# A fused attention and gated feed-forward layer: gate and up multiplied side by side on the two row halves of TensorE, low-rank factors stacked on 96 rows, one background step per attention slot

## The chip, the cores and the metric

One NeuronCore of one Trainium2 chip runs the program. The metric is the device time of one execution in microseconds. Times quoted for the kernel before are those of three timed runs and of one profiled execution.

## What is computed

The input x has 2 x 1024 tokens of width 512, all in float32. Cut to what matters:

```python
xn = _layernorm(x)
# attention: 32 heads of 16 channels, 8 key/value groups, causal
s = softmax(mask(q @ k.T) / 4) @ v @ Wo + bo
# feed-forward, every matrix with a low-rank part of rank 16
gate   = xn @ gate_w.T + (xn @ gate_a.T) @ gate_b.T      # 512 -> 1376
up     = xn @ up_w.T   + (xn @ up_a.T)   @ up_b.T
hidden = silu(gate) * up
g = silu(hidden @ down_w.T + (hidden @ down_a.T) @ down_b.T)
out = x + s * g
```

## The kernel before

Two streams of work are written out for each engine and merged by `interleave`. The *attention* stream goes in slots: 40 slots (`SLOTS`) for each of 16 groups (`N`), a leading round of 40 and 16 last slots. A slot's number within its round decides what stands in it. At each even slot TensorE computes a pair of transposed score tiles `st` (`scores_t`, L887), which ScalarE turns into probabilities `prob` (L1092), one per slot; mostly at even slots it also computes a pair of score tiles `s` (`score_pair`, L868), of which VectorE takes row maxima (L1318, L1321). Both kinds use two matmuls side by side, one on the upper and one on the lower 64 rows of the array. `context` (L904) multiplies probabilities by values, four heads side by side on 32 columns each; it stands at six of the ten slots of a round whose number leaves 2 when divided by 4.

The *background* stream is all the rest, cut into 777 steps (`STEPS`, `TOTAL`). A step of a projection, of gate or up, of down or out is one 128-row tile of the contraction: three matmuls of 128x128 by 128x512 (L197 to L199 in `matmul_hi_lo`), since every operand is split into a high and a low part of type float32r. The stages are: turning x, projections, `b_turn` (the low-rank b factors are transposed), then for each of 11 tiles of hidden rows (`NH`) a `fold` (weights transposed on TensorE, L755, and the product of the low-rank factors added, L759, then split into `w_hi` by ScalarE, L974, and `w_lo` by VectorE, L1173) and `gate` and `up` for each of four chunks of 512 tokens; then `down_fold` (L784, L788), and 16 times `down` (11 steps) and `out` (4 steps). The gate tile is read by `tanh` (ScalarE, L989) and by `gate` (VectorE, L1184); the up tile by `up` (VectorE, L1195), which writes `hid`.

The background has two PSUM banks. A bank goes to units by turn: unit u takes bank u % 2, and `take_bank` waits until unit u - 2 has been read out. So the next gate is computed in one bank while the last up stands in the other.

`interleave` issues an attention slot and then background steps until a quota is met; `MIDDLE` steps are spread evenly over 640 slots (584 steps, 0.91 a slot), after which one step goes with each of the 16 last slots, and the rest follows with no attention beside it. In the second half of the tokens an `out` stands between two `down`s, as in the first half. `load_out` issues nine DMAs on SyncE's queue (L537, L538, L541) into three buffers; `combine` (L1235, L1238), an add on GpSimd (L438) and a store (L545) end a tile.

## Time and profile before

| | |
|---|---|
| median of three runs | 1152.95 us (1144.7 to 1156.6) |
| profiled execution: time, span | 1163.04 us, 1161.2 us |
| granted TensorE clock, mean | 0.923 |
| TensorE busy | 1056.7 us (91%) |
| TensorE weight loads busy | 607.1 us (52%) |
| VectorE busy | 631.7 us (54%) |
| ScalarE busy | 464.8 us (40%) |
| GpSimd busy | 115.3 us (10%) |

The profiled execution is 10 us longer than the median of the timed ones. Weight loads run beside matmuls and are counted apart. A matmul's record runs on after the next has begun, so the distance between two starts is the price of one, not its length.

### The profile page before, as it was taken

The page shows a single profiled execution, that of the slowest core. Times are in us where ns is not written, and L with a number is a line of the kernel's source. Part 1 is how long each engine was busy: PE and PEld are TensorE (multiplying, and loading weights), DVE is VectorE, ACT ScalarE, POOL GpSimd, SP SyncE. Part 2 cuts the span into 40 slices and gives each one's busy share as a digit, 9 for nine tenths or more (in the row PEclk, how much of TensorE's full clock was granted, in tenths as well). Part 3 has the DMA queues.
Part 4 walks back from the last instruction along what each step waited for, and adds up shares of the span by engine and source line. Part 5 has one row for each costly group of instructions (what it writes and reads, how often), then busy time and mean ns, then how long its engine had stood idle before and what let it go on. Part 6 is the DMA issues. An engine that isn't in the chain of part 4 may idle for free.

```text
span 1161.2 us, 16175 instructions
## 1 busy us (share of the span) xinstructions
PE 1056.7 (91%) x5668; PEld 607.1 (52%) x5668; DVE 631.7 (54%) x1752; ACT 464.8 (40%) x917; POOL 115.3 (10%) x159
## 2 busy tenths in 40 slices
PE   4749997999999999999999999999878878799897
PEld 3535453555555555555555555554344434456685
DVE  6636453565655565655665565565545545432344
ACT  3312343544544444444444453444433324353121
POOL 3000000010000101010100000010000101112011
PEclk9979796999999999999999998997678879899899
DMA  6435344131321313130312223124031242133552
GB/s 190 136 108 192 124 148 133 42 91 39 92 75 55 84 36 92 38 87 30 91 54 76 70 60 86 39 75 137 29 95 46 61 115 72 47 102 97 157 166 97
DMA packets 118862, 103.49 MB, mean 89 GB/s; under 512 B 41352, under 2 KB 86408, under 8 KB 118784
## 3 DMA queue, kind: packets, MB, share of 16 engines
q1 hardware_dynamic: 118784, 102.47, 29.5%
q8 instruction: 46, 0.75, 0.3%
q14 instruction: 32, 0.26, 0.1%
HBM read 60.20 MB, written 41.42 MB: 88 GB/s over the span
## 4 chain that ended last, share of the span: by engine, by line
PE 79%; DVE 7%; DMA 5%; ACT 4%; SPq 3%; issue 2%; POOL 0%; POOLq 0%; DVEq 0%; ACTq 0%
PE bank L197 17%; PE o L904 12%; PE bank L198 12%; PE bank L199 12%; PE st L887 11%; PE s L868 8%; DMA q<-scratch_q 2%; PE bank L759 2%; ACT prob L1092 2%; DMA hid_in<-scratch_hid 2%; PE bank L788 1%; PE bank L725 1%; PE bank L755 1%; DVE junk L1318 1%; PE bank L784 1%
## 5 line engine op out<-in xcount | busy, mean ns | idle before, releaser
L1092 ACT ACTIVATE prob<-st 128x512 f32<-128x512 f32 (+1 forms) x640 | 328.1, 551 | 454.6 <-PE st L887 454.2
L1318 DVE CUSTOM_DVE_ANT_0 junk<-s,mask 128x128 bf16<-128x128 f32 (+3 forms) x512 | 230.3, 488 | 208.1 <-PE s L868 207.2
L1321 DVE TENSOR_REDUCE part_max<-s 128x1 f32<-128x512 f32 x256 | 164.8, 686 | 138.6 <-PE s L868 138.4
L868 PE MATMUL s<-k,q 64*128 64x512 f32 (+3 forms) x768 | 153.2, 394 | 42.7 <-DMA q<-scratch_q 25.6
L887 PE MATMUL st<-q,k 64*128 64x512 f32 (+3 forms) x768 | 158.4, 436 | 17.6 <-ACT prob L1092 16.0
L427 POOL TENSOR_SCALAR_AFFINE_SELECT prob<-prob 128x512 f32<-128x512 f32 x128 | 79.8, 635 | 891.3 <-ACT prob L1092 891.3
L197 PE MATMUL bank<-x_hi,w_hi 128*128 128x512 f32 (+1 forms) x352 | 162.7, 462 | 0.0
L904 PE MATMUL o<-prob,v 128*32 128x512 f32 (+3 forms) x1536 | 158.8, 535 | 0.0
L887 PEld LDWEIGHTS st<-q,k 64*128 64x128 f32 x768 | 69.4, 191 | 139.1 <-issue 90.0
L199 PE MATMUL bank<-x_hi,w_lo 128*128 128x512 f32 (+1 forms) x352 | 138.9, 395 | 0.0
L198 PE MATMUL bank<-x_lo,w_hi 128*128 128x512 f32 (+1 forms) x352 | 138.6, 394 | 0.0
L868 PEld LDWEIGHTS s<-k,q 64*128 64x128 f32 x768 | 78.6, 198 | 86.8 <-DVE part_max L1318 30.5
L197 PEld LDWEIGHTS bank<-x_hi,w_hi 128*128 128x128 f32 (+1 forms) x352 | 65.5, 186 | 77.6 <-issue 66.5
L197 PE MATMUL bank<-down_hi,hid_hi 128*128 128x512 f32 (+1 forms) x176 | 80.1, 455 | 7.7 <-DVE ring L1219 5.8
L904 PEld LDWEIGHTS o<-prob,v 128*32 128x32 f32 x1536 | 41.5, 115 | 75.2 <-issue 67.4
L199 PEld LDWEIGHTS bank<-x_hi,w_lo 128*128 128x128 f32 (+1 forms) x352 | 65.4, 186 | 16.1
L198 PE MATMUL bank<-down_lo,hid_hi 128*128 128x512 f32 (+1 forms) x176 | 73.1, 415 | 0.0
L199 PE MATMUL bank<-down_hi,hid_in_lo 128*128 128x512 f32 (+1 forms) x176 | 72.4, 411 | 0.0
L198 PEld LDWEIGHTS bank<-x_lo,w_hi 128*128 128x128 f32 (+1 forms) x352 | 65.7, 187 | 5.4
L197 PEld LDWEIGHTS bank<-down_hi,hid_hi 128*128 128x128 f32 (+1 forms) x176 | 35.3, 200 | 31.4 <-issue 22.4
L1318 DVE DVE_READ_ACCUMULATOR2_ANT part_max<- 128x1 f32 x512 | 42.5, 83 | 0.0
L1184 DVE SCALAR_TENSOR_TENSOR gated<-tanh,bank 128x512 f32<-128x512 f32 (+1 forms) x44 | 30.0, 682 | 21.5 <-ACT tanh L989 21.2
(103 smaller groups left out, 962.1 us busy)
## 6 DMA issues: line engine op xcount, KB each, us to landing
q<-scratch_q SPq DMA_DIRECT2D x64, 200.0 KB
scratch_hid<-hid SPq DMA_DIRECT2D x40, 256.0 KB, 2.1
hid_in<-scratch_hid SPq DMA_DIRECT2D x16, 640.0 KB, 4.3
scratch_q<-proj_hi SPq DMA_DIRECT2D x32, 256.0 KB
scratch_o<-o_sb SPq DMA_DIRECT2D x32, 256.0 KB, 2.1
k<-scratch_k SPq DMA_DIRECT2D x32, 192.0 KB
scratch_q<-proj_lo SPq DMA_DIRECT2D x16, 256.0 KB
ctx<-scratch_o SPq DMA_DIRECT2D x64, 64.0 KB
```

Of the source, the lines that this page charges most:

```text
L197: pe.matmul(out, lhs_hi, rhs_hi, start=start, stop=False)
L198: pe.matmul(out, lhs_hi, rhs_lo, start=False, stop=False)
L199: return pe.matmul(out, lhs_lo, rhs_hi, start=False, stop=stop)
L427: ins = pool.affine_select(out=blk, in_=blk, compare_op=ALU.is_ge, fill=0.0, base=0, pattern=[[0, REP], [1, P]], channel_multiplier=-1)
L759: mm = pe.matmul(out_[:, kt * P:kt * P + hp], a_gu[:, i, kt * P:(kt + 1) * P], bT[:, i, h * P:h * P + hp], start=False, stop=kt == KT - 1, ...
L868: pe.matmul(sb_[(p + odd) % S_BANKS][:, 0:wd], q[half, g % 2, h // 2, qt * P:(qt + 1) * P], k[half, g % 2, k0:k0 + wd], start=True, stop=T ...
L887: mm = pe.matmul(st[odd][:, col:col + q1 - q0], k[half, i % 2, kt * P:(kt + 1) * P], q[half, i % 2, h // 2, q0:q1], start=True, stop=True)
L904: mm = pe.matmul(ob[32 * h:32 * h + 2 * HD, q0 % C:q0 % C + q1 - q0], v[:, i % 3, kt].rearrange("p a e -> p (a e)"), prob[:, job % 3, h, c ...
L1092: nc.scalar.activation(prob[:, job % 3, h, 0:JOB_COLS[j]], st[at % ST_BANKS][:, 0:JOB_COLS[j]], ACT.Exp, scale=float(HD) ** -0.5).then_inc ...
L1184: dve.scalar_tensor_tensor(out=gated[0:hp], in0=th[0:hp], scalar=1.0, in1=bank_of(key)[0:hp, :], op0=ALU.add, op1=ALU.mult).then_inc(gated ...
L1318: ins = dve.tensor_tensor_reduce(junk[:, n % S_BANKS, 0:wd], bank_[:, 0:wd], mask[:, C - wd:C], 1.0, LOWEST, ALU.add, ALU.max, part[:, h, ...
L1321: ins = dve.tensor_reduce(part[:, h, qt, dst:dst + 1], bank_[:, 0:wd], AX.X, ALU.max)
```

## The change

`gate` and `up` of a chunk become one unit `hidden` of eight steps that holds both banks. In the first four steps the upper 64 rows of each contraction tile are multiplied by gate weights into bank 0 while the lower 64 rows are multiplied by up weights into bank 1; in the last four the halves are crossed over. Each step is three pairs of matmuls with 64 rows. ScalarE and VectorE begin to read when all eight steps are done, and `take_bank` of the next unit waits for what was last in its bank or banks (`PRIOR`).

The low-rank factors are loaded three times, at rows 0, 32 and 64 of 96: a as high, low, high and b as high, high, low, so that one float32r matmul with 96 rows gives what one float32 matmul with 16 rows gave. New work for this: a clearing and six copies on GpSimd, `split_a` and `split_b` on ScalarE, `low_a` and `low_b` on VectorE, ten small loads where there were six.

`MIDDLE` is 640 now, one step in each slot, and 69 steps are left behind the middle, where there were 125. VectorE issues a slot's background before its attention. The `out`s of the second half stand behind all `down`s, with `load_out` three tiles ahead.

```diff
@@ bank_order, interleave
-            yield "gate", h, c
-            yield "up", h, c
+            yield "hidden", h, c
...
-        elif t >= NT // 2 + 2:
-            yield "out", t - 2, 0
-    for t in range(NT - 2, NT):
+    for t in range(NT // 2, NT):
         yield "out", t, 0
...
-TAIL = LAST_SLOTS + STEPS["down"] * (NT // 2 - 1) + STEPS["out"] * NT // 2
-MIDDLE = TOTAL - LEAD - EARLY - TAIL
+MIDDLE = SLOTS * N
+TAIL = TOTAL - LEAD - EARLY - MIDDLE
...
+        if kind == "hidden":
+            used = (0, 1)
+        else:
+            used, turn = (turn,), 1 - turn
+        places[kind, a, b] = used
+        prior[kind, a, b] = sorted({last[n] for n in used} - {None})
@@ tensor
             def take_bank(key):
-                u = NUMBER[key]
-                if u >= 2:
-                    pe.wait_ge(*read_out(*KEYS[u - 2]))
-                return bank[u % 2]
+                for u in PRIOR[key]:
+                    pe.wait_ge(*read_out(*KEYS[u]))
+                return bank_of(key)
...
-                for kt in range(KT):
-                    mm = matmul_hi_lo(pe, out_[0:hp, :], wh[:, h % 2, i, kt, 0:hp], wl[:, h % 2, i, kt, 0:hp],
-                                      xh[:, c, kt], xl[:, c, kt], kt == 0, kt == KT - 1)
...
+                take_bank(("hidden", h, c))
+                for cross in range(2):
+                    if cross:
+                        pe.wait_ge(crossed, NCH * h + c + 1)
+                    for kt in range(KT):
+                        for w_, x_ in ((wh, xh), (wl, xh), (wh, xl)):
+                            for odd in range(2):
+                                i = odd ^ cross
+                                half = head_rows(odd, HALF_ROWS)
+                                mm = pe.matmul(bank[i][0:hp, :], w_[half, h % 2, i, kt, 0:hp], x_[half, c, kt],
+                                               start=not cross and kt == 0 and w_ is wh and x_ is xh,
+                                               stop=cross == 1 and kt == KT - 1 and x_ is xl)
...
-                pe.matmul(out_[0:hp, :], a_low[:, h * P:h * P + hp], bT_d[:, :], start=False, stop=True,
+                pe.matmul(out_[0:hp, :], a_d[:, h * P:h * P + hp], bT_d[:, :], start=False, stop=True,
@@ sync
+                for t in range(NT // 2, NT // 2 + 3):
+                    load_out(t)
+                for t in range(NT // 2, NT):
                     yield STEPS["out"]
                     store_out(t)
+                    if t + 3 < NT:
+                        load_out(t + 3)
@@ vector
-            interleave(attention(), background())
+            interleave(attention(), background(), background_first=True)
```

**Where the order moves.** TensorE between one chunk and the next, seventh tile of hidden rows. Before, the up steps (bank1) end and the gate of the next chunk (bank0) begins:

```order
L197 MATMUL bank1<-x_hi,w_hi 128x512
L198 MATMUL bank1<-x_lo,w_hi 128x512
L199 MATMUL bank1<-x_hi,w_lo 128x512
L868 MATMUL s2<-k,q 128x256 [waits s_read]
L868 MATMUL s0<-k,q 128x256
L197 MATMUL bank0<-x_hi,w_hi 128x512 [waits gated_done]
L198 MATMUL bank0<-x_lo,w_hi 128x512
L199 MATMUL bank0<-x_hi,w_lo 128x512
```

The same place now:

```order
L835 MATMUL bank1<-x_lo,w_hi 128x512
L835 MATMUL bank0<-x_lo,w_hi 128x512
L951 MATMUL st0<-q,k 128x512 [waits exp_done]
L951 MATMUL st1<-q,k 128x512
L932 MATMUL s2<-k,q 128x128 [waits s_read]
L932 MATMUL s0<-k,q 128x128
L835 MATMUL bank0<-x_hi,w_hi 128x512 [waits hid_done]
L835 MATMUL bank1<-x_hi,w_hi 128x512
L835 MATMUL bank0<-x_hi,w_lo 128x512
```

The wait before the first matmul of a chunk is now for `hid`, the last reading of the chunk just ended, where it was for the gate reading of that chunk, four steps old; only an `st` pair and an `s` pair (and at some places a `context`) stand between.

ScalarE at the same place, before:

```order
L1092 ACTIVATE prob<-st1 128x512 [waits st_done]
L1110 ACTIVATE o_sb<-o 128x512 [waits sums_landed1,o_stored1,pv_done]
L989 ACTIVATE tanh<-bank0 128x512 [waits gated_done,filled]
L1092 ACTIVATE prob<-st0 128x512 [waits pv_done,st_done]
L1092 ACTIVATE prob<-st1 128x512 [waits st_done]
```

and now:

```order
L1170 ACTIVATE prob<-st1 128x512 [waits st_done]
L1170 ACTIVATE prob<-st0 128x512 [waits st_done]
L1062 ACTIVATE tanh<-bank0 128x512 [waits gated_done,filled]
L1170 ACTIVATE prob<-st1 128x512 [waits st_done]
L1170 ACTIVATE prob<-st0 128x512 [waits pv_done,st_done]
```

The `tanh` stands behind the exponential of `st0`, and that `st0` is the one that TensorE computes after the chunk's last matmul.

VectorE in the last stage, where tiles of the second half are finished. Before, between two `down`s:

```order
L1210 TENSOR_TENSOR hid_in_lo<-hid_in,hid_hi 128x1280 [waits hh_done]
L1211 TENSOR_TENSOR hid_in_lo<-hid_in,hid_hi 96x128
L1219 SCALAR_TENSOR_TENSOR ring<-y_tanh,bank0 128x512 [waits out_stored4,yt_done]
L1224 TENSOR_TENSOR ctx<-ctx,inv_sums 128x512 [waits c_landed2]
L1228 TENSOR_TENSOR ctx_lo<-ctx,ctx_hi 128x512 [waits ch_done]
L1235 TENSOR_TENSOR r1<-bank1,bias 128x512 [waits r2_done,filled]
L1238 SCALAR_TENSOR_TENSOR ring<-r1,ring 128x512 [waits y_done,r1_done]
```

and now, behind the last `down`:

```order
L1315 SCALAR_TENSOR_TENSOR ring<-y_tanh,bank1 128x512 [waits out_stored7,yt_done]
L1320 TENSOR_TENSOR ctx<-ctx,inv_sums 128x512 [waits c_landed2]
L1324 TENSOR_TENSOR ctx_lo<-ctx,ctx_hi 128x512 [waits ch_done]
L1320 TENSOR_TENSOR ctx<-ctx,inv_sums 128x512 [waits c_landed0]
L1324 TENSOR_TENSOR ctx_lo<-ctx,ctx_hi 128x512 [waits ch_done]
L1331 TENSOR_TENSOR r1<-bank0,bias 128x512 [waits r2_done,filled]
L1334 SCALAR_TENSOR_TENSOR ring<-r1,ring 128x512 [waits y_done,r1_done]
L1320 TENSOR_TENSOR ctx<-ctx,inv_sums 128x512 [waits c_landed1]
```

The eight `out`s now follow one another with no `down` (11 steps of TensorE) between them.

## Rows read from the trace of the kernel before

**Rows 1.** The page, part 1: busy time and instructions of each engine.

```profile
PE 1056.7 (91%) x5668; PEld 607.1 (52%) x5668; DVE 631.7 (54%) x1752; ACT 464.8 (40%) x917; POOL 115.3 (10%) x159
```

**Rows 2.** Windows by stage: start:end, length; busy (count) by engine; clock; DMA.

```profile
0.00:106.00 106.00, 67.58 (x335) 50.84 (x335) 62.96 (x168) 29.13 (x53) 9.02 (x15) 0.90 0.48 143
106.00:211.00 105.00, 92.61 (x469) 49.76 (x470) 49.74 (x162) 42.10 (x87) 7.47 (x12) 0.82 0.44 142
211.00:788.00 577.00, 572.58 (x3379) 316.28 (x3379) 346.38 (x1045) 263.64 (x537) 54.16 (x87) 0.99 0.23 66
788.00:842.00 54.00, 50.00 (x191) 20.34 (x191) 29.27 (x74) 25.23 (x45) 2.49 (x4) 0.64 0.29 88
842.00:1061.00 219.00, 186.45 (x930) 99.14 (x929) 101.83 (x251) 85.52 (x168) 27.84 (x31) 0.86 0.27 79
1061.00:1161.20 100.20, 87.46 (x373) 70.75 (x369) 41.48 (x58) 19.14 (x29) 14.27 (x10) 0.95 0.44 134
```

**Rows 3.** Timeline, gate steps and attention: start, duration, engine, line, operands.

```profile
504.39 0.50 PE L197 MATMUL bank<-x_hi,w_hi 128*128 128x512 f32 x1
504.73 0.40 PE L198 MATMUL bank<-x_lo,w_hi 128*128 128x512 f32 x1
504.96 0.40 PE L199 MATMUL bank<-x_hi,w_lo 128*128 128x512 f32 x1
...
505.29 0.50 PE L887 MATMUL st<-q,k 64*128 64x512 f32 x2
505.39 0.19 PEld L868 LDWEIGHTS s<-k,q 64*128 64x128 f32 x2
505.62 0.40 PE L868 MATMUL s<-k,q 64*128 64x512 f32 x2
...
505.95 0.50 PE L197 MATMUL bank<-x_hi,w_hi 128*128 128x512 f32 x1
...
510.34 0.30 PEld L887 LDWEIGHTS st<-q,k 64*128 64x128 f32 x4 [0.36 <-issue]
```

**Rows 4.** Timeline, the readings that follow a filled tile, at two places.

```profile
456.64 0.50 PE L887 MATMUL st<-q,k 64*128 64x384 f32 x4
...
457.18 0.60 ACT L1092 ACTIVATE prob<-st 128x512 f32<-128x512 f32 x1 [1.25 <-PE st L887]
...
457.67 0.59 ACT L989 ACTIVATE tanh<-bank 128x512 f32<-128x512 f32 x1
...
458.30 0.69 DVE L1184 SCALAR_TENSOR_TENSOR gated<-tanh,bank 128x512 f32<-128x512 f32 x1 [1.76 <-ACT tanh L989]
...
789.72 0.68 DVE L1195 SCALAR_TENSOR_TENSOR hid<-gated,bank 96x512 f32<-96x512 f32 x1
...
790.54 0.63 PE L784 MATMUL bank<-ident,ring 128*128 128x128 f32 x4 [0.88 <-DVE hid L1195]
```

**Rows 5.** Timeline, `context` of one block of 256 columns and of two of 512.

```profile
508.18 0.64 PE L904 MATMUL o<-prob,v 128*32 128x256 f32 x8
...
907.43 1.92 PE L904 MATMUL o<-prob,v 128*32 128x512 f32 x16
```

**Rows 6.** Timeline, low-rank products of a fold and of a down fold.

```profile
503.31 1.15 PE L759 MATMUL bank<-bT,a_low 16*128 16x128 f32 x8
...
801.40 1.12 PE L788 MATMUL bank<-bT_d,a_low 16*128 16x512 f32 x2
```

**Rows 7.** Timeline, TensorE behind idle times in the down stage.

```profile
872.21 0.79 PE L868 MATMUL s<-k,q 64*128 64x512 f32 x2 [7.23 <-DVE part_max L1318]
...
918.53 0.73 PE L868 MATMUL s<-k,q 64*128 64x512 f32 x2 [1.81 <-DVE part_max L1318]
```

**Rows 8.** Timeline, loading and readying a tile of the last stage.

```profile
1082.29 0.69 DVE L1224 TENSOR_TENSOR ctx<-ctx,inv_sums 128x512 f32<-128x512 f32 x1 [2.48 <-DMA x_again<-in_L_attn_x]
...
1131.62 0.59 SPq L537 DMA_DIRECT2D ctx<-scratch_o  x1
...
1136.59 0.46 SPq L541 DMA_DIRECT2D x_again<-in_L_attn_x  x1
```

More of the change, by code:

```diff
@@ L94 @@
 PROJECTED += AFTER
-STEPS = dict(turn=1, proj=KT, value=TT, b_turn=1, fold=2, gate=KT, up=KT, down_fold=2, down=NH, out=KT)
+DOWN_LOADED, DOWN_SPLIT, DOWN_TURNED = 1, 3, NH - 1
+STEPS = dict(turn=1, proj=KT, value=TT, b_turn=1, fold=2, hidden=2 * KT, down_fold=2, down=NH, out=KT)
 def bank_order():
@@ L138 @@
 NUMBER = {key: u for u, key in enumerate(KEYS)}
+NUMBER_STEPS = dict(zip(KEYS, accumulate(STEPS[kind] for kind, *_ in KEYS)))
 TOTAL = sum(STEPS[kind] for kind, *_ in NUMBER)
@@ L150, in interleave @@
         done += next(background)
-    for slot, _ in enumerate(attention):
+    if not background_first:
+        next(attention)
+    for slot in range(SLOTS * (N + 1) + LAST_SLOTS):
         if slot < SLOTS:
@@ L159, in interleave @@
             done += next(background)
+        next(attention, None)
     for _ in background:
@@ L444, in background @@
                         add(t - 1)
-                    elif t >= NT // 2 + 2:
-                        yield STEPS["out"]
-                        add(t - 2)
-                for t in range(NT - 2, NT):
+                for t in range(NT // 2, NT):
                     yield STEPS["out"]
@@ L833, in background @@
                     for c in range(NCH):
-                        for i in range(2):
-                            yield from hidden(h, c, i)
+                        yield from hidden(h, c)
                         if c == 1 and h + 1 < NH:
@@ L978, in tanh @@
             def tanh(h, c):
-                key = ("gate", h, c)
+                key = ("hidden", h, c)
                 hp = rows[h]
```

255 lines of the change are left out of this document (162 added, 93 removed).

## The prediction

> **What bounds the kernel now.** I read the busy times first: TensorE is busy for 91% of the span, no other engine for more than 54% [rows 1]. Then the windows by stage [rows 2]: from 211 to 788, the gate and up stage, TensorE is busy 572.6 of 577 us at a clock of 0.99, so there every nanosecond of TensorE counts and every wait of it is new time. From 842 to 1061 (downs beside attention) it is busy 186 of 219 us at 0.86, and there latencies bind. Then the timeline shows what a switch costs [rows 3]. Full-height matmuls follow one another every 0.23 us (504.73 to 504.96). From the last of them to the 64-row `st` pair it takes 0.33 (504.96 to 505.29), from that pair to the next pair 0.33, from the `s` pair back to a full matmul 0.33, and from that first one to the second 0.33. So each change between kinds of tile costs 0.1 us at the end of the old kind and 0.1 at the start of the new. Pair to pair there is no change, and a pair costs what a full matmul does.
>
> **The gate and up stage.** I count it from the order of the program. Before: 1053 full matmuls at 0.228 (240 us); 514 attention pairs of 384 columns on the average, at 0.18 (93); 129 context groups at 0.66 (85), from 0.64 less two changes for 256 columns and 0.86 for 512 [rows 5]; 20 folds at 0.44 for the turning and 1.08 for the low-rank product [rows 6] (30); 2 us of turned maxima. That is 450. The stage has 577, of which 4.4 are idle and 6 lost to the clock; the other 117 are spread on 604 changes of kind, 0.19 each, as the rows say.
>
> After, the same stage has 1054 pairs in place of the full matmuls. A pair in a row of pairs has no row here longer than two; I bound it between 0.21 (512 columns as fast as they stream) and 0.33 (nothing overlapped), and take 0.228, since the loads for the `s` pair start at 505.39, 0.1 us into the `st` pair, and four loads for two pairs end within 0.30 us [rows 3]: 240 us. Attention, with 47 fewer slots of it in this stage since a slot now carries a whole step: 466 pairs (84), 116 groups (77). Folds: the product on 96 rows lies between 0.23 and the old 1.08; I take 0.44, the price of the four transposes, which also use 128 columns each: 18 us. Maxima 2. Changes of kind: 187 are left in the order, at 0.19: 35. Sum 456.
>
> **The new wait.** A chunk holds both banks, so the next one waits until the last reading of this one is over. The order shows what stands between: `st`, `s`, at some places `context`. The chain of readings, from the start of that `st` pair [rows 4]: exponential after 0.54 (0.43 where no change stands ahead), `tanh` 0.49 later (the exponential stands before it on ScalarE), gate 0.63 later, 0.69 for it, `hid` 0.68 and 0.14 until TensorE starts (789.72 to 790.54). Sum 3.06 us. Against this TensorE has 0.3 to 0.6 us of pairs, and 0.6 to 1.9 of context where there is one. Of 44 ends of a chunk, 16 have only pairs: 2.6 us of idle each, 41 us. Four have the context of 256 columns: 1.7 each, 7. The other 24 have longer ones: 13 together. Behind a fold the chain is shorter by one reading (2.4 us), and 11 such places add 9. Together 70 us. Queued behind that wait are all later `st` and `s` pairs, so ScalarE and VectorE wait too, but both have room. With 5 us of the old idle time the stage comes to 531.
>
> **The clock.** At 918.53, behind 1.81 us of idle, the `s` pair takes 0.73 instead of 0.40 [rows 7, 3]: TensorE went from 2.4 to 1.2 GHz, and what it does in such a stretch takes twice as long; I price one fall at 1.7 us. The new 2.6 us waits are longer. Against that speaks that dense pairs stand around them. I take six of ten of the 16 bare waits (16 us) and 10 us for the folds, where waits and transposes come together: 26, between 0 (no fall) and 55 (one at each of 33 places). Stage after: 556, before 577.
>
> The Trainium skill, "TensorE: Matmul & The Clock Gate", in "Why this matters for your kernels", warns only of idle gaps longer than the waits I forecast; by it this term would be nil. The trace has a fall behind a shorter gap, so the term stays.
>
> **The other stages.** Up to 106 nothing changes. Projections (106 to 211): five slots of attention fewer, 1 us each: 100. Down folds (788 to 842, clock 0.64): 11 products fall from 1.05 [rows 6] to 0.23 at full clock, 9 us, and to 15 with the clock as it is there: 39. Downs beside attention: 173 steps instead of 117, so 168 more matmuls (38 us), 56 more pairs (10), 14 more groups (9), 65 more changes (12). By the same prices the stage before had 162 us of work in 219, so 57 were lost for 8.6 tiles: ScalarE and VectorE stand in order behind the landing of `hid_in`, at worst 7.23 us [rows 7]. Now 12.4 tiles, the later ones with fewer duties; I add 18, between 0 and 25. VectorE's background ahead of its attention may help or harm there; nothing excludes either, and I take 0 of a band of 15 each way. Stage after: 219 + 69 + 18 = 306.
>
> **The end.** Behind the last context (1061) before: 100 us for 123 steps. After: 35 steps are left, but how they follow matters. Three tiles are loaded ahead; each of the other five loads takes 5.4 us of SyncE's queue (1131.62 to 1137.05) and 0.44 for the store ahead of it, lands 2.3 us later, and then takes 2.1 us in VectorE and ScalarE before its `out` [rows 8]. Before, this hid beside 10 us of down and out; now one `out` is 2.7 us of TensorE and hides nothing. Following the queue, the last store ends 54 us behind the last down: first free load at 9.6, five loads at 5.9 to 7 each to 41, landing and readying 4.4, out 2.7, combine, add and store 6. The 21 to 24 us of downs ahead: 78 in all, between 60 (loads hidden) and 85 (outs at half clock).
>
> **Sum.** 106 + 100 + 556 + 39 + 306 + 78 = 1185 against a span of 1161: +2.0%. New work outside TensorE (a clearing and six small copies on GpSimd, splits of a and b) I cost at nothing: it is spread over projection slots with GpSimd at 7 of 105 us and ScalarE at 42 of 105 [rows 2]; uncovered it would be some 5 us, once. The profiled execution was 10 us over the median, so I scale the median: 1153 x 1.020 = 1177.
>
> **Rivals.**
> - *The waits are hidden* and the changes of kind decide: place, the 55 ends of chunks and folds. Each hundredth of a us of average wait is 0.55 us, and with the clock 0.75. The balance turns faster than 1% where the average wait is below some 0.8 us instead of 1.27, that is, where the chain is near 2.2 us. For it: ScalarE and VectorE are at half load. Against: the order puts an exponential before each `tanh`, and each link has its row. Time: 1185 less 50 to 60, scaled 1120 to 1130. Chance 0.14.
> - *The clock holds* at full speed, or the down stage gains from VectorE's order: 1185 less 25, scaled 1152. Chance 0.15.
> - *It falls at almost every wait* and the last outs run slow as well: 1185 plus 35, scaled 1212. Chance 0.12.
> - *Pairs in a row don't overlap* their loads: 1054 times 0.1 us, 1290 in span. The loads of [rows 3] speak against it. Chance 0.03. The Trainium skill, in the same page under "Part 3: Packing small matmuls", says that a weight load overlaps a running matmul only where the row groups differ, which would bring this about; here loads for the same rows start under a running pair.
> - *The change doesn't do what it says*, matmuls of the two halves running one after another: excluded by pairs at 0.33 us including a change.
> The forecast itself has 0.56.
>
> **Numbers.** Within 1% of the median is about what the timing can't tell from no change. Faster by over 1%: 0.15; within: 0.16; slower: 0.69. The range leaves out the ends of the first and the whole of the fourth rival: 1128 to 1213.
>
> **What would show it.** Idle times before the first pair of a chunk released by `hid`, 2.4 to 2.7 us at bare places; 0.23 us from pair to pair; less than 0.1 us at a start of `st` behind a hidden pair; clock of the stage near 0.93; a tail of nearly 80 us with TensorE under 60% busy and SyncE's loads back to back. It is wrong if the chain is broken somewhere by an earlier read, if the clock keeps at 1.0, or if the stage with downs loses less than before.

## The result, and the profile after

| | before | after |
|---|---|---|
| median | 1154.8 us (1144.7 to 1159.8, 4 runs) | 1263.8 us (1261.6 to 1268.9, 4 runs) |
| ratio to before | | 1.0975, 95% interval 1.0918 to 1.1032 |
| profiled span | 1161.2 us | 1263.9 us |
| granted clock, mean | 0.923 | 0.881 |

The change makes the kernel 9.8% slower. The sign was forecast, the size was not: 1177 predicted, and 1264 lies 51 us beyond the upper end of the range. The page's part 1 of the kernel after answers to [rows 1]; VectorE, ScalarE and GpSimd do what they did within 10 us each, and TensorE is now busy for 82%.

```profile
PE 1033.7 (82%) x6625; PEld 660.3 (52%) x6625; DVE 641.6 (51%) x1761; ACT 463.9 (37%) x919; POOL 122.8 (10%) x171
```

Windows of the kernel after, cut at the same places of the program as [rows 2] (start, projections, gate and up, down folds, downs beside attention, end):

```profile
0.00:113.00 113.00, 73.47 (x347) 53.92 (x347) 66.65 (x174) 29.08 (x53) 10.60 (x17) 0.88 0.46 142
113.00:220.00 107.00, 81.24 (x390) 44.13 (x391) 45.87 (x137) 37.37 (x76) 11.00 (x19) 0.80 0.44 132
220.00:820.00 600.00, 523.87 (x4207) 357.42 (x4205) 328.08 (x969) 244.72 (x500) 50.01 (x80) 0.91 0.21 60
820.00:863.00 43.00, 33.14 (x162) 17.27 (x162) 29.87 (x79) 24.26 (x45) 1.86 (x3) 0.72 0.37 102
863.00:1175.00 312.00, 262.96 (x1320) 143.41 (x1324) 143.39 (x363) 117.63 (x229) 38.77 (x44) 0.89 0.26 74
1175.00:1263.90 88.90, 59.04 (x209) 44.20 (x201) 27.78 (x41) 10.85 (x17) 10.57 (x8) 0.82 0.38 114
```

Gate and up take 600 us at a clock of 0.91, where 556 were predicted; the down stage, at 312, was forecast at 306. The view of waits, TensorE alone, names what it waited for (total, times, longest):

```profile
PE bank L835 <- DVE hid L1291: 45.5, 29, 2.7
...
PE bank L810 <- DVE hid L1291: 15.5, 9, 2.6
```

Both lines are the new wait behind a chunk, 61 us together: L835 is the next chunk's first pair, L810 the first transpose of a fold. The timeline of one such place answers to [rows 4]:

```profile
510.59 0.39 PE L951 MATMUL st<-q,k 64*128 64x512 f32 x2
...
511.02 0.60 ACT L1170 ACTIVATE prob<-st 128x512 f32<-128x512 f32 x1 [0.73 <-PE st L951]
...
511.51 0.59 ACT L1062 ACTIVATE tanh<-bank 128x512 f32<-128x512 f32 x1
...
512.13 0.69 DVE L1282 SCALAR_TENSOR_TENSOR gated<-tanh,bank 128x512 f32<-128x512 f32 x1 [1.42 <-ACT tanh L1062]
...
512.86 0.69 DVE L1291 SCALAR_TENSOR_TENSOR hid<-gated,bank 128x512 f32<-128x512 f32 x1
...
513.60 0.50 PE L835 MATMUL bank<-x_hi,w_hi 64*128 64x512 f32 x2 [1.82 <-DVE hid L1291]
```

From the `st` pair to the next chunk's first pair: 3.01 us, predicted 3.06. Between the two stands a `context` of 256 columns, so 1.82 us of that time are idle. And this is what a pair costs, with another kind of pair behind it and at either clock:

```profile
508.54 0.40 PE L835 MATMUL bank<-x_lo,w_hi 64*128 64x512 f32 x2
508.55 0.19 PEld L951 LDWEIGHTS st<-q,k 64*128 64x128 f32 x2
508.78 0.39 PE L951 MATMUL st<-q,k 64*128 64x512 f32 x2
509.01 0.39 PE L932 MATMUL s<-k,q 64*128 64x512 f32 x2
509.23 0.39 PE L835 MATMUL bank<-x_hi,w_hi 64*128 64x512 f32 x2
...
516.71 0.63 PE L835 MATMUL bank<-x_lo,w_hi 64*128 64x512 f32 x2
517.13 0.63 PE L835 MATMUL bank<-x_hi,w_hi 64*128 64x512 f32 x2
```

The distance between starts is 0.23 us, whatever pair follows, and 0.42 to 0.43 three us behind the wait above. TensorE fell from 2.4 to 1.2 GHz there. Over the stage I counted in the trace, between the first fold and the last gate or up matmul: idle time between matmuls 75 us (before 4), and 107 us at half clock in 19 stretches (before 10 us in 2). A stretch at half clock costs half its length, so that is 54 us lost. One of the 19 came over from the projections, where it began behind 4.72 us of idle time; it costs 6 us. The other 18 are falls within the stage, and they are of two sorts, as two windows show (the granted clock is the third number from the end):

```profile
600.10:603.50 3.40, 3.40 (x20) 2.66 (x18) 1.29 (x2) 1.08 (x2) 0.00 (x0) 0.51 0.22 78
641.10:651.30 10.20, 10.20 (x52) 7.14 (x51) 3.79 (x17) 3.47 (x8) 1.22 (x2) 0.50 0.35 106
```

The first is behind a wait between two chunks, and 12 of the 18 are as short: 1.7 us lost each, 20 in all. The second runs through a fold. There are 6 of the longer sort, 5 through a fold and one right behind one: 3.4 to 5.1 us lost each, 27 in all. Thirteen of the 18 follow the 16 waits that have only pairs before them (2.0 to 2.65 us of idle), two follow waits with one short `context` (1.8 and 1.9), and three come at the first chunk behind a fold, after several waits of 0.3 to 1.6. Length alone doesn't decide: a wait of 2.37 us brought no fall, and the one of 1.82 above brought one.

The end of the program answers to [rows 8]. SyncE's queue, then TensorE:

```profile
1203.60 0.39 PE L226 MATMUL bank<-down_hi,hid_in_lo 96*128 96x512 f32 x1
...
1215.69 0.60 SPq L590 DMA_DIRECT2D ctx<-scratch_o  x1
...
1223.83 0.69 DVE L1320 TENSOR_TENSOR ctx<-ctx,inv_sums 128x512 f32<-128x512 f32 x1 [6.74 <-DMA x_again<-in_L_attn_x]
...
1226.01 0.77 PE L224 MATMUL bank<-wo_hi,ctx_hi 128*128 128x512 f32 x1 [7.18 <-issue]
1226.58 0.63 PE L225 MATMUL bank<-wo_lo,ctx_hi 128*128 128x512 f32 x1
```

A load issued from 1215.69 to 1221.1 is used by TensorE at 1226.01, after 7.18 us of idle time, and what follows runs at half clock. From the last `down` (1203.6) to the end are 60 us, predicted 54.

### The profile page after: what moved, and what is told of

Same layout as the page of the kernel before. It is cut to its first block, busy times and chain, and to the rows that moved or that the text cites. A ratio compares the mean times of both kernels' runs of the same rounds, so it can differ in the third digit from the quotient of the medians.

```text
span 1263.9 us, 18154 instructions
## 1 busy us (share of the span) xinstructions
PE 1033.7 (82%) x6625; PEld 660.3 (52%) x6625; DVE 641.6 (51%) x1761; ACT 463.9 (37%) x919; POOL 122.8 (10%) x171
## 4 chain that ended last, share of the span: by engine, by line
PE 68%; DVE 12%; ACT 6%; issue 6%; DMA 5%; SPq 2%; POOLq 0%; ACTq 0%; DVEq 0%
PE bank L835 22%; PE o L968 9%; PE st L951 7%; PE s L932 7%; PE bank L224 7%; PE bank L225 5%; PE bank L226 5%; DVE gated L1282 2%; DVE hid L1291 2%; DMA hid_in<-scratch_hid 2%; ACT tanh L1062 2%; PE bank L781 1%; DMA q<-scratch_q 1%; DVE hid_in_lo L1306 1%; DMA scratch_q<-proj_lo 1%
## 5 line engine op out<-in xcount | busy, mean ns | idle before, releaser
L932 PE MATMUL s<-k,q 64*128 64x512 f32 (+3 forms) x768 | 160.9, 407 | 65.4 <-DVE part_max L1420 24.8
L835 PE MATMUL bank<-x_hi,w_hi 64*128 64x512 f32 (+1 forms) x704 | 160.3, 441 | 51.0 <-DVE hid L1291 45.5
L951 PE MATMUL st<-q,k 64*128 64x512 f32 (+3 forms) x768 | 147.6, 403 | 32.7 <-ACT prob L1170 32.5
L835 PE MATMUL bank<-x_lo,w_hi 64*128 64x512 f32 (+1 forms) x704 | 150.0, 411 | 0.0
L835 PE MATMUL bank<-x_hi,w_lo 64*128 64x512 f32 (+1 forms) x704 | 149.8, 410 | 0.0
L835 PEld LDWEIGHTS bank<-x_hi,w_hi 64*128 64x128 f32 (+1 forms) x704 | 74.2, 196 | 99.9 <-DVE hid L1291 42.5
L951 PEld LDWEIGHTS st<-q,k 64*128 64x128 f32 x768 | 77.4, 200 | 91.8 <-ACT prob L1170 45.5
L835 PEld LDWEIGHTS bank<-x_lo,w_hi 64*128 64x128 f32 (+1 forms) x704 | 73.7, 194 | 13.8
L835 PEld LDWEIGHTS bank<-x_hi,w_lo 64*128 64x128 f32 (+1 forms) x704 | 74.7, 197 | 7.8
L224 PE MATMUL bank<-wo_hi,ctx_hi 128*128 128x512 f32 x64 | 33.1, 516 | 21.9 <-issue 21.9
```

The costliest lines, as they stand in the source:

```text
L224: pe.matmul(out, lhs_hi, rhs_hi, start=start, stop=False)
L835: mm = pe.matmul(bank[i][0:hp, :], w_[half, h % 2, i, kt, 0:hp], x_[half, c, kt], start=not cross and kt == 0 and w_ is wh and x_ is xh, s ...
L932: pe.matmul(sb_[(p + odd) % S_BANKS][:, 0:wd], q[half, g % 2, h // 2, qt * P:(qt + 1) * P], k[half, g % 2, k0:k0 + wd], start=True, stop=T ...
L951: mm = pe.matmul(st[odd][:, col:col + q1 - q0], k[half, i % 2, kt * P:(kt + 1) * P], q[half, i % 2, h // 2, q0:q1], start=True, stop=True)
```

## Experiments

A run was timed beside the kernel before, and its ratio is to that: the median of the kernel before went from 1153.5 to 1161.1 us between such comparisons. All stage figures in this table are counted in each run's profiled execution for the gate and up stage: its length, TensorE's idle time between matmuls, half of its time at half clock ("clock"), and the rest, which is work. Idle time within a half-clock stretch, up to 11 us, is counted on both sides, so "clock" is up to 5 us too high and work as much too low. The last column is the length of what comes from the first `down` to the end.

| kernel | median | stage | idle | clock | work | downs + end |
|---|---|---|---|---|---|---|
| before | 1153.5 to 1161.1 | 582 | 4 | 5 | 573 | 320 |
| after | 1263.8 | 600 | 75 | 54 | 471 | 401 |
| b_low96 | 1154.7 | 579 | 10 | 7 | 562 | 318 |
| a_separate | 1229.5 | 566 | 17 | 11 | 538 | 404 |
| a_full_height | 1319.2 | 660 | 81 | 53 | 526 | 401 |
| a_fill | 1254.3 | 589 | 37 | 15 | 537 | 407 |
| a_vector_old | 1272.1 | 622 | 93 | 63 | 466 | 393 |
| a_tail_old | 1295.0 | 701 | 115 | 89 | 497 | 326 |
| a_pace_old | 1321.2 | 702 | 116 | 90 | 496 | 353 |
| a_tanh_first | 1214.3 | 544 | 42 | 25 | 477 | 418 |
| a_firsts_inside | 1190.9 | 543 | 42 | 25 | 476 | 393 |
| a_copy | 1163.9 | 514 | 28 | 9 | 477 | 397 |
| a_aligned | 1283.4 | 691 | 121 | 82 | 488 | 322 |
| a_best | 1234.0 | 647 | 98 | 53 | 496 | 317 |
| a_best_copy | 1181.3 | 614 | 74 | 41 | 499 | 314 |
| a_context | 1159.6 | 582 | 64 | 19 | 499 | 314 |
| a_context_firsts | 1128.3 | 565 | 43 | 25 | 497 | 315 |
| a_context_copy | 1127.3 | 557 | 33 | 26 | 498 | 315 |

Work is 466 to 477 wherever chunks are paired at one step per slot (a_fill, with its added pairs, apart), and 488 to 499 at the old pace: it hardly moves with the order. What moves is idle time and clock.

**a_full_height: the wait without the pairs**

```diff
-                for cross in range(2):
-                    if cross:
-                        pe.wait_ge(crossed, NCH * h + c + 1)
...
+                for i in range(2):
+                    for kt in range(KT):
+                        mm = matmul_hi_lo(pe, bank[i][0:hp, :], wh[:, h % 2, i, kt, 0:hp], wl[:, h % 2, i, kt, 0:hp],
+                                          xh[:, c, kt], xl[:, c, kt], kt == 0, kt == KT - 1)
```

> The changed kernel, but a chunk's matmuls are 128 rows high again: gate into one bank, then up into the other; the chunk still holds both banks and is read only when all eight steps are done. The wait stays, the pairs go. Theory (a change between kinds of tile costs 0.19 us, and the wait is there besides): the 417 changes saved in the gate and up stage come back, 79 us, and some of them at half clock: 1335 to 1350 us, the stage near 670 us, idle time before the first matmul of a chunk as now. Rival (the changes cost nothing next to the waits, the pairs gain nothing): within 1% of the changed kernel, 1250 to 1276 us.

Measured: 1319.2 us, ratio to before 1.149 (1.138 to 1.160). Windows of this run, gate and up:

```profile
215.00:874.40 659.40, 578.23 (x3146) 320.58 (x3144) 328.33 (x969) 244.43 (x499) 49.82 (x80) 0.92 0.19 55
```

That is 16 us under the expected range. Idle time and clock loss are those of the kernel after; the work is 55 us more. So the pairs are a gain, and the wait is not their doing. The trace has 558 changes of kind in this stage and the kernel after 195, so by this run one is worth 0.15 us and not 0.19. By a_separate below, with the same 363 changes more and 67 us more work, it is 0.18; how to divide the rest between changes and other costs is left open.

**a_separate: the rest of the change without the joint chunk.** Gate and up are again two units of four steps with 128-row matmuls, each in one bank by turn.

```diff
-            yield "hidden", h, c
+            yield "gate", h, c
+            yield "up", h, c
```

> The changed kernel with gate and up as before: two units of four steps of 128-row matmuls, each in its own bank by turn; all else of the change stays. Theory: the gate and up stage loses its 74 us of waits and nearly all of its 49 us of clock loss and gets back 79 us of changes of kind, so 1264 - 74 - 45 + 79 = 1224, 1210 to 1235. Rival (the paired matmuls are no loss, the rest of the change is): 1264 or more.

Measured: 1229.5 us, 1.061 (1.055 to 1.068). Windows: gate and up, downs beside attention, end.

```profile
215.00:781.00 566.00, 548.85 (x3149) 306.07 (x3148) 324.57 (x971) 244.74 (x500) 49.62 (x80) 0.98 0.22 64
822.00:1137.00 315.00, 265.05 (x1325) 143.97 (x1325) 143.03 (x363) 117.72 (x230) 38.72 (x44) 0.88 0.26 73
1137.00:1225.70 88.70, 58.06 (x201) 43.90 (x200) 27.76 (x41) 10.69 (x17) 10.56 (x8) 0.81 0.37 114
```

As expected within 6 us. The joint chunk costs 34 us here: 67 less work against 58 more idle time and 43 more clock loss. The rest of the loss, 64 us by the spans, is in the rest of the change: from the first `down` on it takes 404 us, against 320 before, while the stage of gate and up is 16 shorter than before, the down folds 13, and what comes ahead of the first fold 9 longer.

**b_low96: the kernel before with the 96-row low-rank factors.** The kernel after with the units, the pace, the orders of outs and of VectorE as before.

```diff
-                pe.matmul(out_[0:hp, :], a_low[:, h * P:h * P + hp], bT_d[:, :], start=False, stop=True,
+                pe.matmul(out_[0:hp, :], a_d[:, h * P:h * P + hp], bT_d[:, :], start=False, stop=True,
```

> The kernel before with the low-rank factors three times on 96 rows and nothing else of the change. Theory: 22 folds lose 0.4 to 0.6 us each and 11 down folds 0.8 to 1.2 (the float32 products on 16 rows took 1.08 and 1.05), together 18 to 26 us: 1129 to 1137. Rival (the product was hidden behind what a fold waits for, and the new splits of a and b take the gain in the projections): 1150 to 1160.

Measured: 1154.7 us (10 runs), 1.0036 (0.9996 to 1.0076): no gain, as the rival had it. The products did get cheaper: work in the gate and up stage falls by 11 us, and the down folds go from 54 to 42. Windows, gate and up and the down folds:

```profile
215.00:794.00 579.00, 568.51 (x3322) 310.18 (x3320) 350.55 (x1054) 267.65 (x544) 54.68 (x90) 0.99 0.23 66
794.00:836.00 42.00, 32.52 (x179) 16.03 (x178) 29.38 (x73) 24.70 (x45) 2.49 (x4) 0.79 0.39 113
```

Against it stand 8 us more up to the first fold (214 against 206) and 8 us of idle time and clock in the gate and up stage. In these profiles the span is 7.6 us shorter all the same, and the timed medians don't show it (the profiled execution of before was 8 to 10 us over its median); which of the two small losses is real is left open.

**a_fill: TensorE kept at work in the wait.** At 20 ends of a chunk with little behind them the score pair is computed over again.

```diff
+                for n_ in range(2 * (again // wd)):
+                    odd = n_ % 2
+                    half = head_rows(odd, HALF_ROWS)
+                    pe.matmul(sb_[(p + odd) % S_BANKS][:, 0:wd], q[half, g % 2, h // 2, qt * P:(qt + 1) * P],
+                              k[half, g % 2, k0:k0 + wd], start=True, stop=True)
```

> The changed kernel with extra work in its waits: at 20 ends of a chunk behind which TensorE has little to do, the score pair that stands there is computed over again, 5120 columns (3072 where a short context stands there too), some 2.2 (1.3) us at full speed; the last copy alone signals, so the result is that of one. Theory (the clock falls because TensorE idles; in the stage 97 us now run at 1.2 GHz, which costs 48): the falls behind those ends go, the clock of the stage rises from 0.92 to 0.96 or more, and the time falls by 15 to 30 us, to 1234 to 1249. Rival (the falls come from something else, from folds or from the change of work): the added work runs in part at half clock and outlasts the wait, 1264 to 1300.

Measured: 1254.3 us, 1.093 (1.084 to 1.102), 9.5 less than the kernel after. Windows, gate and up:

```profile
213.00:802.00 589.00, 551.45 (x5049) 393.61 (x5049) 329.84 (x973) 244.82 (x499) 50.20 (x81) 0.97 0.21 62
```

The clock rises from 0.91 to 0.97 and the half-clock stretches go from 19 to 7 (in either, one of them came over from the projections) although TensorE does 66 us more: the other 12 came from the idle time behind chunks, and their price, 39 us, is recovered. The time falls by less than was expected because copies with few columns take longer than was reckoned: of the added pairs those of 512 columns follow one another every 0.23 us and those of 128 every 0.11, so that 5120 columns in pairs of 128 are 4.4 us and outlast the wait.

**a_vector_old: VectorE's old order**

```diff
-            interleave(attention(), background(), background_first=True)
+            interleave(attention(), background())
```

> The changed kernel with VectorE's old order: a slot's attention before its background. Theory (the new order makes VectorE wait for a projection's high part before it reads score maxima, 35 us of such waits in the trace after, and TensorE waits for those readings): projections 117 to about 105, downs beside attention 313 to about 300, and at the chunks the maxima stand ahead of gate, 0.3 us more at 44 ends, +10: together 1245 to 1255. Rival (the order only moves VectorE's own idle time): 1264 within 5, or up to 1280 if the maxima lengthen every chain.

Measured: 1272.1 us, 1.110 (1.098 to 1.122), 8 more than the kernel after. That is in the rival's second range, where the maxima lengthen the chains; outside the chunks the theory has it. Windows: projections, gate and up, downs beside attention.

```profile
111.00:209.00 98.00, 72.09 (x387) 39.05 (x383) 45.36 (x135) 37.15 (x76) 10.97 (x19) 0.88 0.48 147
209.00:832.00 623.00, 530.72 (x4208) 366.49 (x4208) 331.30 (x970) 244.64 (x500) 48.47 (x80) 0.90 0.20 58
871.00:1175.00 304.00, 256.55 (x1325) 140.27 (x1325) 144.06 (x363) 117.80 (x229) 40.05 (x44) 0.91 0.26 76
```

Outside the chunks the new order costs 9 us in the projections and 8 beside the downs, where 12 and 13 were expected, and 4 in the down folds (39 us here). Inside it saves 22, twice what I gave it: with maxima ahead of `gate` idle time goes from 75 to 93 us and clock loss from 54 to 63. In the profiled executions the two sides balance (spans of 1263.9 and 1263.4 us); the 8 us stand in the medians alone.

**a_tail_old and a_pace_old: the pace and the order of the outs**

```diff
-MIDDLE = SLOTS * N
-TAIL = TOTAL - LEAD - EARLY - MIDDLE
+TAIL = LAST_SLOTS + STEPS["down"] * (NT // 2 - 1) + STEPS["out"] * NT // 2
+MIDDLE = TOTAL - LEAD - EARLY - TAIL
```

> The changed kernel with the old pace (584 background steps over the 640 slots) and the old order of the outs (each between two downs). Theory (the steps moved into the slots come where latencies bind, and the loads of the last eight outs are bare): gate and up 590 to about 620 (47 more slots of attention in it), downs beside attention 313 to about 230, end 89 to about 100: 1215 to 1230. Rival (the work only moves, each step costs the same wherever it stands): 1255 to 1270.

> The changed kernel with the old pace alone; the outs of the second half still stand behind all downs. Theory (the pace costs most of what the last two stages lost, the order of the outs the rest, since nothing hides SyncE's five loads of 5.4 us each): 10 to 25 us slower than with the old outs as well, so 1230 to 1245. Rival (the order of the outs costs nothing, because downs before them no longer wait): the same as with both old, within 5 us.

Measured: a_tail_old (with the outs between the downs again) 1295.0 us, 1.117 (1.110 to 1.124); a_pace_old (outs behind all downs) 1321.2, 1.142 (1.134 to 1.151). Windows of a_tail_old (gate and up, downs, end), then of a_pace_old (downs, end):

```profile
221.00:922.00 701.00, 585.45 (x4378) 379.97 (x4374) 353.75 (x1052) 267.28 (x543) 54.87 (x90) 0.87 0.19 55
968.00:1195.00 227.00, 189.83 (x933) 101.42 (x932) 100.58 (x252) 85.77 (x168) 27.02 (x32) 0.85 0.26 76
1195.00:1294.00 99.00, 85.96 (x368) 69.68 (x366) 41.31 (x57) 18.71 (x29) 14.16 (x10) 0.96 0.46 136
```
```profile
965.00:1192.00 227.00, 187.91 (x931) 100.26 (x932) 100.66 (x252) 85.41 (x168) 26.81 (x31) 0.86 0.26 76
1192.00:1317.60 125.60, 93.75 (x369) 73.50 (x368) 41.43 (x58) 19.11 (x29) 14.27 (x10) 0.91 0.36 107
```

The outs behind all downs cost 26 us, all of it at the end, about as expected (10 to 25). Downs and end were forecast too (227 + 99). But the stage of gate and up, forecast at 620, took 701, and so both expectations fell: with chunks that hold both banks, the new pace alone (a_pace_old against the kernel after) is worth 102 us in the stage and costs 49 from the first `down` on; the new order of the outs costs the other 26. By the order, 20 of the 44 chunks of a_tail_old end ahead of an odd slot, where no `st` pair stands behind them (behind 12 there is nothing at all, behind 8 an `s` pair), and 3 have a `context` behind them; in the kernel after it is none and 28. The old order of the outs at the new pace wasn't tried: there a tile's loads would wait for results of attention that stand behind it in the order.

**a_tanh_first and a_firsts_inside: a shorter chain**

```diff
@@ scalar
-            interleave(attention(), background())
+            interleave(attention(), background(), background_first=True)
```

> The changed kernel with ScalarE issuing a slot's background before its attention, as VectorE does, so that tanh stands ahead of the exponential. Theory (the wait of a chunk is the chain of readings, and the exponential is 0.4 to 0.9 us of it): the first pair of a chunk starts 0.5 us or more earlier at 44 ends, 22 us less idle and fewer clock falls, but projections and downs may lose up to 10: 1235 to 1250. Rival (the exponential that is late holds up context and the next st pair): 1264 to 1285.

Measured: 1214.3 us, 1.048 (1.041 to 1.055), 50 less than the kernel after, where 14 to 29 were expected. The timeline behind a chunk's end:

```profile
453.74 0.41 PE L951 MATMUL st<-q,k 64*128 64x512 f32 x2
...
453.95 0.60 ACT L1062 ACTIVATE tanh<-bank 128x512 f32<-128x512 f32 x1 [0.68 <-PE bank L835]
...
454.58 0.69 DVE L1282 SCALAR_TENSOR_TENSOR gated<-tanh,bank 128x512 f32<-128x512 f32 x1 [0.99 <-ACT tanh L1062]
455.31 0.69 DVE L1291 SCALAR_TENSOR_TENSOR hid<-gated,bank 128x512 f32<-128x512 f32 x1
...
456.05 0.50 PE L835 MATMUL bank<-x_hi,w_hi 64*128 64x512 f32 x2 [1.68 <-DVE hid L1291]
```

`tanh` starts beside the `st` pair of 453.74 and not behind its exponential; the chain from that pair is 2.31 us where it was 3.01. Idle time goes from 75 to 42 us, clock loss from 54 to 25. a_firsts_inside confines this order, on both engines, to the slots of gate and up:

```diff
+        held = first_in_hidden and FIRST_HIDDEN < due <= LAST_HIDDEN
+        while issued < slot + (0 if held else 1):
+            next(attention, None)
+            issued += 1
```

> The changed kernel with ScalarE and VectorE issuing background first while gate and up run, and attention first in all other stages. Theory (the order is worth its 56 us on ScalarE and 22 on VectorE only where a chunk waits to be read; elsewhere it delays the exponential, for which the next st pair waits): gate and up as with tanh first, 544; projections about 99, downs 331 to about 305: 1180 to 1197. Rival (outside, the order does nothing and the stages differ by chance): 1210 to 1220.

Measured: 1190.9 us, 1.037 (1.027 to 1.046), as expected: downs beside attention take 304 us again and not 330, the projections 98.

**a_aligned: chunks end ahead of even slots.** The quota of steps is a table that lets each chunk end ahead of an even slot, at the old pace on the average.

```diff
+            slot = SLOTS - 1 + (end - LEAD - EARLY) * SLOTS * N / MIDDLE
+            points.append((2 * round((slot - 1) / 2) + 1, end))
...
-            due = LEAD + EARLY + MIDDLE * (slot + 1 - SLOTS) // (SLOTS * N)
+            due = QUOTA[slot]
```

> The changed kernel with the old pace and the old order of the outs, but the quota of steps is bent so that every chunk ends just ahead of an even slot, as it does at one step per slot (8 or 10 slots for a chunk where the plain old pace ends chunks anywhere). Theory (one step per slot is worth its 100 us in the gate and up stage because the chunk's end then always meets the score pairs, whose exponential and maxima run beside the readings; where it ends ahead of an odd slot TensorE has nothing): idle time of the stage 115 to about 75, half-clock time 178 to about 100, stage 701 to 625, with downs 227 and end 100 as they are: 1215 to 1230. Rival (it is the pace itself, more attention between steps, that costs): 1280 to 1295.

Measured: 1283.4 us, 1.116 (1.106 to 1.127). The theory fell: 10 us of the 100 came back. The time is in the range of the rival, the pace itself; a_context below keeps that pace and is 124 us faster, so it isn't the pace itself either. Its waits, TensorE's:

```profile
PE bank L860 <- DVE hid L1317: 74.5, 33, 3.1
PE bank L835 <- DVE hid L1317: 24.8, 10, 3.1
```

**a_best and a_best_copy: both ideas on the wrong alignment.** a_best is a_aligned with a_firsts_inside's order; a_best_copy adds a copy of `up` by ScalarE, for which the next chunk waits in place of `hid`:

```diff
+                nc.scalar.activation(hid[0:hp, n % 3], bank[1][0:hp, :], ACT.Copy).then_inc(up_copied, 1)
```

> Both together: the bent old pace, the old order of the outs, and background first on ScalarE and VectorE while gate and up run. Theory (sum of the stages as other runs had them: 110 + 100 + 570 + 42 + 220 + 100): 1142, 1132 to 1155, at or a little under the kernel before. Rival (longer chunks in slots bring more score pairs that wait, and the stage keeps 600): 1170 or more.

> The same, and ScalarE copies the up tile out of its bank into the hid buffer behind tanh, so that the next chunk waits for gate and for this copy, not for hid. Theory (the last reading, 0.68 us, leaves the chain of every chunk, and a copy of 0.5 to 0.6 runs beside gate): 0.6 us less idle at 30 to 40 ends and fewer falls of the clock, 20 to 30 us: 1112 to 1125. Rival (the copy stands ahead of the exponential, and the next st pair waits for that): no gain, 1140 to 1160.

Measured: 1234.0 us, 1.072 (1.063 to 1.082), and 1181.3, 1.028 (1.018 to 1.038). Both sums rested on the alignment that had failed and missed by 92 and some 60 us; 1234.0 is in the first one's rival's range (1170 or more), and 1181.3 above both ranges of the second. The copy was worth 53 by the medians and 40 by the profiled spans; 24 us of that are idle time and 12 clock loss of the stage.

**a_context: chunks end ahead of a context.** A `context` stands behind 28 of the 44 ends in the kernel after, behind 7 in a_aligned and behind all 44 here, counted from the order.

```diff
-            points.append((2 * round((slot - 1) / 2) + 1, end))
+            points.append((8 * round((slot - 5) / 8) + 5, end))
```

> As the run with chunk ends ahead of even slots, but bent so that each chunk ends ahead of a slot with a context behind its score pairs (the eight slots 6, 14, 22, 30 and 38 of a round, counted from the order; at one step per slot, 28 of the 44 ends meet one, at the old pace and in the aligned run about half or fewer do). Theory (what the new pace is worth in the gate and up stage is the context that fills the wait): idle time of the stage from 121 to 60 or less, half-clock time from 164 to under 90, stage 691 to 600 or less: 1180 to 1215. Rival (the pace itself): 1270 to 1285.

Measured: 1159.6 us (10 runs), 1.0027 (0.9991 to 1.0062): 20 us under the expected range, 124 less than a_aligned by one line of the quota, and equal to the kernel before. TensorE in the two runs, a_aligned, then a_context:

```profile
300.77 0.39 PE L978 MATMUL st<-q,k 64*128 64x512 f32 x2
...
303.78 0.79 PE L860 MATMUL bank<-x_hi,w_hi 64*128 64x512 f32 x2 [2.39 <-DVE hid L1317]
```
```profile
334.84 0.44 PE L978 MATMUL st<-q,k 64*128 64x512 f32 x2
...
335.43 1.92 PE L995 MATMUL o<-prob,v 128*32 128x512 f32 x16
337.84 0.50 PE L860 MATMUL bank<-x_hi,w_hi 64*128 64x512 f32 x2 [0.49 <-DVE hid L1317]
```

The chain is as long in both, 3.01 and 3.00 us from the `st` pair; in the second 1.92 us of it are work that has to be done anyway. Half-clock time in the stage fell from 164 to 38 us.

**a_context_firsts, a_context_copy, a_copy.** The same with the order of a_firsts_inside; with the copy as well; and that order with the copy at the pace and the outs of the kernel after.

> The same, with background first on ScalarE and VectorE while gate and up run. Theory: the wait of an end falls by a further 0.5 to 0.8 us, under the context there: 1145 to 1175, idle of the stage under 35. Rival (context waits for the exponential that is now late, and the gain is lost again): 1190 or more.

> The same, and ScalarE's copy of the up tile in place of hid in the chain. Theory (another 0.6 us where anything is left to take): 1125 to 1155, at or under the kernel before. Rival (nothing is left to take, and the copy delays the exponential): as without it or up to 15 us slower.

> One step per slot and the new order of the outs as in the changed kernel, background first on ScalarE and VectorE while gate and up run, and ScalarE's copy of the up tile. Theory: 21 waits of 1.3 us and 7 at folds go nearly away, 30 of 42 us of idle time and most of the 25 us of clock loss, against 1191 without the copy: 1150 to 1170. Rival (the copy moves the wait to the st pairs): 1190.

Measured: a_context_firsts 1128.3 us, 0.9766 (0.9702 to 0.983), faster than both kernels and below what was expected; a_context_copy 1127.3, 0.9751 (0.9688 to 0.9814), so where a context stands the copy adds nothing that the medians show (the stage is 8 us shorter in the profile); a_copy 1163.9, 1.0106 (1.0065 to 1.0147), as expected. Windows of a_context_firsts: gate and up, downs beside attention, end.

```profile
210.00:775.00 565.00, 521.38 (x4359) 345.30 (x4355) 349.66 (x1040) 264.22 (x536) 53.65 (x88) 0.96 0.23 67
818.00:1033.00 215.00, 181.01 (x937) 97.61 (x935) 103.86 (x253) 87.00 (x172) 29.07 (x33) 0.89 0.28 80
1033.00:1132.90 99.90, 87.14 (x373) 70.61 (x369) 41.52 (x58) 19.23 (x30) 14.30 (x10) 0.97 0.44 135
```

The stage of gate and up beats that of before by 17 us, and downs and end cost no more than there. That is the version to keep. Where its gain over the kernel before comes from is not taken apart further: the stage has 76 us less work, 39 more idle time and 20 more clock loss.

## Why the prediction was right and wrong

The predicted sum was 1185 us in terms of the span, and the span is 1263.9. By the windows above the 79 us are: start +7, projections +7, gate and up +44, down folds +4, downs beside attention +6, end +11.

- *The wait behind a chunk* (chain 3.06 us, 70 us of waits and 5 of old idle time): right, without luck: chain 3.01, idle time of the stage 75, and the places as well, 28 ends with a `context` and 16 without.
- *The clock* ("I price one fall at 1.7 us", 26 us in all, 0 to 55): the step that failed. It measured 54 us, 28 more than the term and the upper end of its bound. The price of 1.7 us was right for 12 falls, 20 us in all, where 16 stood for the bare waits. It was wrong at the folds: 6 falls in or right behind one cost 27 us, 4.5 each, where "10 us for the folds" stood. And the 6 us of a stretch that reaches in from the projections had no term. Thirteen of the 16 bare waits were followed by a fall where six of ten had been taken. a_fill shows the mechanism: with work in the waits 12 of the stretches are gone. Why a fall in a fold lasts longer wasn't tested; a_full_height has three of the longer sort with no fold in them, so the fold is not the whole reason.
- *The price of a change of kind* (0.19 us, 456 us of work): right in mechanism, and the work is 471, 15 us of the 44. The changes themselves are not what was missing: at 0.15 to 0.18 us their term of 35 would be 29 to 35. Counted from start to start, with the changes among them, gate and up pairs take 253 us, attention pairs 107, contexts 86, folds 22 and maxima 5, where 240, 84, 77, 18 and 2 were priced beside the 35. The prediction had laid on the changes all that its prices left of the stage before, 117 us, and some of that stayed when the changes went. How much is which is left open.
- *Pairs in a row* at 0.23 us with loads that overlap: right, and so the fourth rival is out. The Trainium skill, "TensorE: Matmul & The Clock Gate", in "Part 3: Packing small matmuls", would have had loads for the same rows wait; the rows at 508.54 to 509.23 don't show that: the loads for the `st` pair start 0.01 us behind the pair before it, and the pairs keep their 0.23. Its warning in "Why this matters for your kernels" names gaps longer than these, and by it the clock term was nil: the measurement decides against it here, by the 48 us of the 18 falls that follow waits of at most 2.65. The same page's section "A second HAM failure mode: psum-queue depth-cycling", which I had not weighed, says that short idle times that recur between groups of matmuls, as PSUM banks go round, make the clock swing between its two levels; the 18 falls in a stage whose chunks take both banks agree with it.
- *The start and the projections* ("nothing changes", 100 us): wrong by 14. a_vector_old gives 9 in the projections and 2 at the start back to VectorE's order, which had a band of 15 in the down stage and no term here, and b_low96 has 8 us from the low-rank work, costed "at nothing" with 5 as its worst. Together they are more than the 14, so they don't simply add up; how they share it wasn't tested.
- *The down stage* (306): right within 6. In part that is luck: VectorE's order, taken at 0, costs 8 there, as a_vector_old has 304, so the other terms together were 2 too high.
- *The down folds* (39): 43.
- *The end* (last store 54 us behind the last down, 78 in all): the queue of loads was read rightly, 60 us behind the last down and 26 of them a loss by a_pace_old against a_tail_old. The missing 11 are 5 in the downs ahead of them (28.6 us for 21 to 24) and 6 behind. There the first free load stood 12.1 us behind the last down and not 9.6, and the last out took 5.1 us and not 2.7; both the first out, ahead of that load, and the last one ran at half clock, as did 32 us of the last 89. The words "35 steps are left" leave out the 32 steps of the outs, which the sum has.
- *The scaling* by 1153/1163: the profiled execution after stood at its median, so another 8 of the 87 us between 1177 and 1264 come from there.

Of the rivals "it falls at almost every wait and the last outs run slow as well" (1212) comes nearest to what happened at the bare waits and in the end, with 35 us for it where 79 came, and a chance of 0.12. The others did not occur: the waits were not hidden, the clock did not hold. All six stages came out long, which a range built from terms that err either way doesn't cover. One reason is plain, that idle time brings falls with it; that the terms as a whole were tied is argued, not shown.

The prediction also read the pace as a plain transfer of steps between stages. That did the forecast no harm, since it counted the ends of chunks as the new pace places them. But the runs show the pace as part of the joint chunk's price: it puts 28 contexts behind the chunks' ends, and a_context, with 44, is 124 us faster than a_aligned, with 7.

## What to carry to other kernels

When a unit takes all buffers and the next one must wait for its last reading, what decides is which independent work the order puts behind its end: one line of a quota moved this kernel by 124 us, and the chain's order on the reading engines by 50. Price such a wait as idle time plus the clock falls that come with it (54 us for 75 here; 0.3 to 0.8 of the idle time in the runs with joint chunks), with a price of its own for a fall at each kind of place, and look at where the pace of two streams lets the ends fall before counting instructions saved. And where a change has five parts, cost each against the others: here the pace, a gain of 102 us for one part, cost 49 elsewhere, and placing the ends of chunks had that gain without the price.

## What the runs showed of the hardware

- A pair of 64-row matmuls of 512 columns follows another pair every 0.23 us, whatever tiles they belong to (508.54 to 509.23), as fast as a full-height matmul of the kernel before [rows 3]; a change of kind costs 0.15 to 0.18 us on the average (55 and 67 us for 363 changes, a_full_height and a_separate).
- Pairs in a row of 128 columns follow one another every 0.11 us (median in a_fill), half the 0.23 us of pairs with four times the columns. A single `st` pair of 128 columns is followed by the next `s` pair after 0.06 us (median of 28 in the kernel after), so the 0.11 is the pace of many in a row.
- In the gate and up stage of the kernel after, whose waits are at most 2.65 us each, TensorE fell to 1.2 GHz 18 times, 95 us in all: 12 times at 1.7 us lost, and 6 times, in a fold or right behind one, at 3.4 to 5.1. With copies of a score pair in 20 of the waits it fell 6 times, 20 us in all, though its busy time rose from 524 to 551 us.
- The low-rank product with 96 rows of float32r in place of 16 of float32 took the down folds from 54 to 42 us, and changed the time of the whole by nothing that can be measured.
